# Softmax division moved from the rows of P to the weighed values in PSUM, with the prologue and the loads in another order

## The chip, the cores and the metric

The kernel runs on one core of one Trainium2 chip. The metric is the device time of one execution in microseconds (us), as the median of several runs. A profiled execution has a span, from its first to its last instruction, and a time of its own, a little longer than the span.

## The reference

`x` is 1024 rows (tokens) of 512 numbers. What is computed, cut to what matters:

```python
xn = _layernorm(x)                                     # 1024 x 512
qkv = xn @ w_qkv.T                                     # 32 query heads in 8 groups of 4, 8 key and 8 value heads, 128 wide
scores = einsum('bskgd,btkd->bkgst', qh, kh) / sqrt(128)
scores = where(causal, scores, finfo.min)
probs = softmax(scores, axis=-1)
attn = einsum('bkgst,btkd->bskgd', probs, vh)
s = attn.reshape(B, S, 4096) @ w_dense.T               # 1024 x 512
g = silu(ffn(xn))                                      # three 512 x 512 layers of weights +1 and -1
return x + s * g
```

## The kernel before, in words

Every fp32 product is made of three matmuls of fp32r parts: a value is split into a hi part (a rounding copy, by ACT) and a lo part (the value minus hi, by DVE or POOL), and `three` (lines 1074 to 1079) adds hi·hi, hi·lo and lo·hi. So each result that goes into another matmul is read by ACT (hi) and then by DVE or POOL (lo).

The work is in 8 groups, one for each key head with its 4 query heads. The program is a prologue (layer norm, its transposes, the projections of group 0 for the first 512 tokens, the first row block of scores), a loop of 7 bodies, and a last group, which also holds the feed-forward layers and the output. Each engine has its own list of items, run strictly in order: `prologue()`, `BODY` and `LAST` give those lists for PE (TensorE), ACT, DVE, POOL and SP, the queue that issues all DMAs. Semaphores tie the lists together. Nothing is scheduled at run time. An engine that waits holds up everything behind it in its list.

The items of a body, for 8 row blocks i of 128 tokens:

- `unit.p.half.c`: a quarter of a projection (q0 to q3, k, v), three matmuls of 512 columns into one of two shared PSUM banks. `split.p` makes the hi and lo parts of a loaded weight piece of 256 KB (lines 863 to 876, POOL 739 to 748); `load.p` brings it into a ring of 5 slots. The pieces are q0 to q3, k, v and wd0 to wd3 (`w_dense`).
- `scores.i.r`: scores of 32 tokens times 4 heads (128 rows) against the keys up to there, 32 to 1024 columns; r is 0 to 3. `max.i.r` (DVE, 927) masks them, negates them and takes the row's extreme; `exp.i.r` (ACT, 789) writes the row tile to `prob_even` or `prob_odd` and its sum to `row_sum`.
- `inverse.i.r` (DVE, 936) is the reciprocal of the sums; `norm.i.r` multiplies the tile by it in place: tiles 0 and 1 on ACT (798), 2 and 3 on POOL (729).
- `flip.i` (DVE, 945) transposes the 32 x 32 blocks. DMAs then bring the row block, tokens along the free dimension, into `pt_lo`: rows 1 to 3 and 8 by way of DRAM (`dw`, 640, and `dr`, 652), rows 4 to 7 by 16 small DMAs within SBUF (`move`, 663). Row 8 is row block 0 of the next group; the prologue makes it for group 0. `LAND_AFTER` says how many pairs must have been weighed before the slots of a row may be overwritten.
- `land.i.j`: hi (ACT, 833) and lo (POOL, 737; five pairs of a group on DVE, 996) of one 128 x 512 piece of P.
- `weigh.i.j` (PE): that piece times the values, added up over j in `ps_o`. `hi.weigh.i` (ACT, 839) and `lo.weigh.i` (DVE, 1009) split the sum; `dense.i.h` (PE) multiplies it by the piece of `w_dense`, and `lo.dense.i` (DVE, 1042) adds the product to `y`.

In the prologue POOL zeroes all of `y` (line 750, 128 x 4096). The last group ends with `dense.7`, its add into `y`, `gate.7`, `add_x.7` and the output DMA.

Of the kernel before, what the change touches and what calls it, by code (L numbers as in the profile page):

```python
# [123 lines left out]
def parse(tokens):  # L125


    def item(words):
# [4 lines left out]
    return [item(token.split(".")) for token in tokens.split()]


def prologue():
# [7 lines left out]
    pe = ln(0, 1, 2, 3) + unit("q0") + unit("q1") + ln(4, 5) + unit("q2") + ln(6, 7) \  # L144
        + unit("q3") + unit("k") + unit("v") + [("scores", first, r) for r in tiles] + values
# [18 lines left out]
    sp = [("load", p) for p in PIECES] + [("scales",), ("dw", first), ("dr", first)]
# [11 lines left out]
        dense.0.2 dense.0.3 scores.5.0 scores.5.1 weigh.2.1 weigh.2.2 unit.q2.0.0 unit.q2.0.1
        unit.q2.0.2 scores.5.2 scores.5.3 unit.q2.0.3 dense.1.0 dense.1.1 dense.1.2 scores.6.0
        dense.1.3 vblocks.1 weigh.3.0 weigh.3.1 weigh.3.2 weigh.3.3 scores.6.1 dense.2.0 dense.2.1
        dense.2.2 weigh.4.0 scores.6.2 weigh.4.1 scores.6.3 dense.2.3 weigh.4.2 unit.q0.0.0
        scores.7.0 scores.7.1 weigh.4.3 unit.q0.0.1 weigh.4.4 unit.q0.0.2 weigh.5.0 scores.7.2  # L180
        unit.q0.0.3 unit.q1.0.0 unit.q1.0.1 weigh.5.1 scores.7.3 weigh.5.2 unit.q1.0.2 unit.q1.0.3
# [12 lines left out]
        exp.3.3 norm.3.0 hi.unit.q3.1 norm.3.1 hi.land.1.0 hi.land.1.1 hi.split.q3 hi.split.v
        hi.weigh.0 hi.land.2.0 exp.4.0 hi.land.2.1 exp.4.1 hi.land.2.2 hi.weigh.1 norm.4.0 exp.4.2
        exp.4.3 norm.4.1 hi.split.k exp.5.0 exp.5.1 hi.weigh.2 hi.land.3.0 hi.land.3.1 hi.land.3.2
        hi.land.3.3 exp.5.2 hi.unit.q2.0 exp.5.3 norm.5.0 norm.5.1 hi.vblocks.1 hi.weigh.3
        hi.land.4.0 exp.6.0 hi.land.4.1 exp.6.1 hi.land.4.2 hi.land.4.3 hi.land.4.4 norm.6.0
# [143 lines left out]
class Run:  # L342
# [907 lines left out]
```

## Time and profile before

| | |
|---|---|
| device time, median of 3 runs | 947.64 us (946.23 to 949.11) |
| profiled execution: its own time | 945.07 us |
| profiled execution: span | 943.4 us |
| mean granted clock of TensorE | 0.991 |
| instructions | 15763 |
| start to start of two bodies | 106.9 us |

The profile gives each engine's busy time, a table by stretches of time, the waits with the engine that ended them, and a timeline of instructions. In a timeline row the first number is the start, the second how long it took; a matmul's length contains the filling of a pipeline, so that the distance from one start to the next tells what it costs. A bracket holds the idle time of the engine before the row and what ended it. SPq is the queue of SP, with the issues of DMAs.

### The profile page before, as it was taken

The numbers are of one execution on the slowest core, as the hardware profiler recorded it, in microseconds if no ns is written. First come the engines' busy times: TensorE is split into PE (matmuls) and PEld (weight loads), VectorE is DVE, ScalarE is ACT, GpSimd is POOL, SyncE is SP. The second block draws the span as 40 slices with busy tenths as digits, with TensorE's granted clock in tenths as the row PEclk, the third lists the DMA queues.
The fourth block names the chain that finished last, engine by engine and source line by source line (L and its number), as shares of the span: only waits on it lengthen the run. The fifth ranks groups of instructions, "written<-read, shape, count | busy, mean of one in ns | idle before, by whom it ended". The sixth has DMA issues, their size and how long they took to land.

```text
span 943.4 us, 15763 instructions
## 1 busy us (share of the span) xinstructions
PE 909.3 (96%) x4272; PEld 758.4 (80%) x4272; DVE 639.8 (68%) x1291; ACT 583.8 (62%) x1205; POOL 613.1 (65%) x500
## 2 busy tenths in 40 slices
PE   6879999999999999999999999999999999999997
PEld 5768777888788877888788877888788877888785
DVE  8447755787667765786667765777567775598646
ACT  3368654776558754777558664778457664656733
POOL 6058665677558764678467774678467774466947
PEclk9879999999999999999999999999999999999999
DMA  4066454755447454655447545555537546344335
GB/s 156 12 177 176 103 124 116 193 137 124 111 124 198 112 117 128 181 142 128 105 124 202 120 103 141 167 145 128 115 111 213 122 90 155 101 138 107 80 90 179
DMA packets 185463, 124.84 MB, mean 132 GB/s; under 512 B 12896, under 2 KB 161888, under 8 KB 185440
## 3 DMA queue, kind: packets, MB, share of 16 engines
q1 hardware_dynamic: 185440, 124.57, 51.3%
q8 instruction: 10, 0.16, 0.1%
q14 instruction: 13, 0.11, 0.0%
HBM read 46.93 MB, written 23.07 MB: 74 GB/s over the span
## 4 chain that ended last, share of the span: by engine, by line
POOL 41%; issue 40%; PE 10%; DVE 3%; SPq 2%; DMA 1%; ACT 1%; POOLq 1%; DVEq 0%; ACTq 0%
POOL pt_lo L737 23%; POOL prob_odd L729 5%; POOL w_lo L747 5%; POOL prob_even L729 4%; POOL wd_lo L747 3%; SPq L663 2%; PE ps_m L1209 2%; PE ps_m L1077 2%; PE ps_m L1078 2%; PE ps_m L1079 2%; PE ps_s L1077 1%; PE ps_s L1078 1%; PE ps_s L1079 1%; PE ps_o L1077 1%; DVE half_var L901 0%
## 5 line engine op out<-in xcount | busy, mean ns | idle before, releaser
L737 POOL TENSOR_TENSOR pt_lo<-pt_lo,pt_hi 128x512 fp32r<-128x512 f32 x248 | 332.7, 1366 | 117.1 <-ACT pt_hi L833 115.7
L927 DVE CUSTOM_DVE_ANT_0 ps_s<-ps_s,mask 128x32 f32<-128x32 f32 (+31 forms) x256 | 182.0, 714 | 102.9 <-PE ps_s L1079 98.3
L833 ACT ACTIVATE pt_hi<-pt_lo 128x512 fp32r<-128x512 f32 x288 | 170.0, 626 | 77.2 <-PE ps_o L1079 23.1
L1077 PE MATMUL ps_m<-xn_hi,w_hi 128*128 128x512 f32 (+1 forms) x388 | 153.3, 395 | 0.7 <-DVE xn_lo L1002 0.7
L1078 PE MATMUL ps_m<-xn_lo,w_hi 128*128 128x512 f32 (+1 forms) x388 | 151.8, 391 | 0.0
L1079 PE MATMUL ps_m<-xn_hi,w_lo 128*128 128x512 f32 (+1 forms) x388 | 151.6, 391 | 0.0
L1077 PE MATMUL ps_s<-k_hi,q_hi 128*128 128x480 f32 (+15 forms) x384 | 125.5, 327 | 9.2 <-ACT prob_odd L789 9.1
L1077 PE MATMUL ps_o<-pt_hi,v_hi 128*128 128x512 f32 x288 | 119.1, 413 | 8.8 <-POOL pt_lo L737 7.6
L1078 PE MATMUL ps_s<-k_lo,q_hi 128*128 128x480 f32 (+15 forms) x384 | 127.3, 332 | 0.0
L1079 PE MATMUL ps_s<-k_hi,q_lo 128*128 128x480 f32 (+15 forms) x384 | 127.1, 331 | 0.0
L729 POOL TENSOR_TENSOR prob_even<-prob_even,row_inv 128x96 f32<-128x96 f32 (+3 forms) x64 | 64.6, 1020 | 96.0 <-DVE row_inv L936 95.7
L789 ACT ACTIVATE prob_odd<-ps_s,neg_max 128x160 f32<-128x160 f32 (+15 forms) x128 | 95.8, 751 | 38.7 <-DVE neg_max L927 37.8
L789 ACT ACTIVATE prob_even<-ps_s,neg_max 128x32 f32<-128x32 f32 (+15 forms) x128 | 82.5, 645 | 56.5 <-DVE neg_max L927 52.7
L1078 PE MATMUL ps_o<-pt_lo,v_hi 128*128 128x512 f32 x288 | 113.0, 392 | 0.0
L1079 PE MATMUL ps_o<-pt_hi,v_lo 128*128 128x512 f32 x288 | 112.9, 392 | 0.0
L1077 PE MATMUL ps_m<-wd_hi,at_hi 128*128 128x512 f32 x256 | 100.4, 392 | 0.9 <-DVE at_lo L1009 0.9
L729 POOL TENSOR_TENSOR prob_odd<-prob_odd,row_inv 128x224 f32<-128x224 f32 (+3 forms) x64 | 77.8, 1235 | 35.5 <-DVE row_inv L936 35.5
L1078 PE MATMUL ps_m<-wd_lo,at_hi 128*128 128x512 f32 x256 | 99.9, 390 | 0.0
L1079 PE MATMUL ps_m<-wd_hi,at_lo 128*128 128x512 f32 x256 | 99.8, 390 | 0.0
L945 DVE STREAM_TRANSPOSE prob_odd<-prob_odd 128x1024 f32<-128x1024 f32 (+1 forms) x80 | 95.4, 1222 | 0.0
L1077 PEld LDWEIGHTS ps_s<-k_hi,q_hi 128*128 128x128 f32 x384 | 72.8, 190 | 19.6 <-ACT prob_odd L789 10.0
L1079 PEld LDWEIGHTS ps_m<-xn_hi,w_lo 128*128 128x128 f32 x388 | 73.4, 189 | 15.8
(103 smaller groups left out, 1624.4 us busy)
## 6 DMA issues: line engine op xcount, KB each, us to landing
pt_lo<-prob_odd SPq DMA_DIRECT2D x128, 128.0 KB, 2.4
pt_lo<-prob_even SPq DMA_DIRECT2D x128, 112.0 KB, 2.3
raw<-wqkv SPq DMA_DIRECT2D x48, 256.0 KB, 2.9
pt_lo<-prob_odd SPq DMA_DIRECT2D x128, 96.0 KB, 2.2
pt_lo<-prob_even SPq DMA_DIRECT2D x128, 80.0 KB, 2.1
raw<-wd SPq DMA_DIRECT2D x32, 256.0 KB, 3.5
turned<-prob_odd SPq DMA_DIRECT2D x32, 256.0 KB, 4.0
pt_lo<-turned SPq DMA_DIRECT2D x8, 1024.0 KB, 5.5
```

The source lines that it names most:

```text
L663: sp.dma_start(pt_lo[b * Q:(b + 1) * Q, slots, h * P:(h + 1) * P].bitcast(F32), prob_quadrants(i)[h * Q:(h + 1) * Q, :, b, :])\
L729: pool.tensor_tensor(rows, rows, row_inv[:, slot:slot + 1, None].to_broadcast([P, width(i % BLOCKS, tile) // Q, Q]), ALU.mult).then_inc(no ...
L737: pool.tensor_tensor(pt_lo[:, slot, :], pt_lo[:, slot, :].bitcast(F32), pt_hi[:, hi_slot, :], ALU.subtract).then_inc(land_lo, 1)
L747: pool.tensor_tensor(lo, raw[:, r.raw_slot(piece), :], hi, ALU.subtract)\
L789: act.activation(prob_tile(i, tile), as_tiles(score_row(i, tile)), ACT.Exp, scale=-1.0, bias=neg_max[:, slot:slot + 1], accum_out=row_sum[ ...
L833: act.activation(pt_hi[:, hi_slot, :], pt_lo[:, LAND_AT[i % BLOCKS] + j, :].bitcast(F32), ACT.Copy).then_inc(land_hi, 1)
L927: dve.tensor_tensor_reduce(out=scores, in0=scores, in1=mask[:, S - width(i % BLOCKS, tile):S], scale=-1.0, scalar=BIG, op0=ALU.add, op1=AL ...
L945: dve.transpose(rows, rows).then_inc(flipped, 1)
L1077: pe.matmul(out, sta_hi, mov_hi, start=start, stop=False)
L1078: pe.matmul(out, sta_hi, mov_lo, start=False, stop=False)
L1079: return pe.matmul(out, sta_lo, mov_hi, start=False, stop=stop)
L1209: mm = pe.matmul(bank[:, :], ffn_w[layer][c][:, o * P:(o + 1) * P], ffn_in(layer, part, c, half), start=(c == 0 and part == 0), stop=(c == ...
```

## The change

The rows of P are no longer normalized. `norm` is gone from ACT and POOL, 32 items a group. `inverse.i` is one reciprocal of the four sums of a row block. Its 128 x 4 result is written by `rw.i` to the DRAM tensor `inv`, and `rr.i` reads the 512 numbers back into each of the 128 partitions (`inv_rows`). A new DVE item, `mul.weigh.i`, multiplies the weighed sum in `ps_o` by them in place, before `hi.weigh.i` and `lo.weigh.i`. `flip.i` now waits for the row's four `exp` items alone.

```diff
-    if what == "norm":                                  (ACT; the same on POOL, as a tensor_tensor)
-        act.wait_ge(inverse_done, r.score_no(i, tile))
-        act.activation(rows, rows, ACT.Copy, scale=row_inv[:, slot:slot + 1])
-    dve.wait_ge(exp_done, r.score_no(i, tile))
-    dve.reciprocal(row_inv[:, slot:slot + 1], row_sum[:, slot:slot + 1])
+    dve.wait_ge(exp_done, r.score_no(i, TILES - 1))
+    dve.wait_ge(inv_written[i % 2], INV_WRITTEN0 + r.inv_writes(i) - 16)
+    dve.reciprocal(row_inv[:, stat_slots(i)], row_sum[:, stat_slots(i)])
+elif what == "rw":
+    sp.wait_ge(inverse_done, r.row_no(i))
+    sp.wait_ge(inv_landed, INV_LANDED0 + 16 * r.row_no(i - 2))
+    sp.dma_start(inv_d[i % 2, :, :], row_inv[:, stat_slots(i)])
+elif what == "rr":
+    sp.wait_ge(inv_written[i % 2], INV_WRITTEN0 + r.inv_writes(i))
+    sp.wait_ge(attn_scaled, r.row_no(i - 1))
+    sp.dma_start(inv_rows[:, :], inv_d[i % 2, :, :].rearrange("p r -> (p r)").partition_broadcast(P))
+if what == "mul":
+    dve.wait_ge(block_weighed, WEIGHED0 + PAIRS * g + tri(i + 1))
+    dve.wait_ge(inv_landed, INV_LANDED0 + 16 * r.row_no(i))
+    dve.tensor_tensor(weighed_f32(i).rearrange("p h (r c) -> p h r c", c=Q),
+        ps_o[i % 2][:, :].rearrange("p (h r c) -> p h r c", r=TILES, c=Q),
+        inv_rows[:, :].rearrange("p (h c r) -> p h r c", c=Q, r=TILES), ALU.mult)
-    act.wait_ge(block_weighed, WEIGHED0 + PAIRS * g + tri(i + 1))     (hi.weigh)
+    act.wait_ge(attn_scaled, BLOCKS * g + i + 1)
```

In the prologue POOL zeroes only the first of the 8 blocks of `y`, at its very start, and a DMA copies it to the other seven. Query projection q2 comes ahead of the transposes of blocks 4 and 5, q3 ahead of those of 6 and 7. The pieces wd0 to wd3 of a group are loaded at the end of the group before (in the prologue for group 0).

```diff
-    pe = ln(0, 1, 2, 3) + unit("q0") + unit("q1") + ln(4, 5) + unit("q2") + ln(6, 7) + unit("q3") + unit("k") + unit("v")
+    pe = ln(0, 1, 2, 3) + unit("q0") + unit("q1") + unit("q2") + ln(4, 5) + unit("q3") + ln(6, 7) + unit("k") + unit("v")
-        pool.memset(y[:, :, :], 0.0)
+        pool.memset(y[:, 0, :], 0.0).then_inc(y_zero, 1)
+        sp.wait_ge(y_zero, 1)
+        sp.dma_start(y[:, 1:BLOCKS, :], y[:, 0:1, :].to_broadcast([P, BLOCKS - 1, E])).then_inc(y_zero, 16)
-    sp = [("load", p) for p in PIECES] + [("scales",), ("dw", first), ("dr", first)]
+    sp = [("load", p) for p in PIECES + [f"wd{h}" for h in range(HEADS)]] + [("scales",), ("dw", first), ("rw", first), ("dr", first), ("rr", first)]
```

The tables `BODY` and `LAST` are written anew for all five engines. The head of PE's table for a body shows how:

```diff
-        scores.1.0 unit.q2.1.0 scores.1.1 scores.1.2 unit.q2.1.1 scores.1.3 unit.q2.1.2 scores.2.0
+        scores.1.0 scores.1.1 unit.k.1.0 scores.1.2 scores.1.3 unit.k.1.1 scores.2.0 unit.k.1.2
```

Three places of the order, before and after (line numbers are those of each kernel). The first is SP at the end of the prologue, up to the first weight loads of the loop. Before:

```order
L632 DMA scales<-s 128x1 x3
L640 DMA turned<-prob_even 32x4x128 x4
L652 DMA pt_lo<-turned 128x512
L671 UNCONDITIONAL_BRANCH
L671 ISA
L628 ISA
L628 DMA raw<-wd 128x512
```

With the change:

```order
L629 DMA raw<-wd 128x512 x4
L634 DMA y<-y 128x7x512
L637 DMA scales<-s 128x1 x3
L660 DMA turned<-prob_even 32x4x128 x4
L644 DMA inv<-small 128x4
L672 DMA pt_lo<-turned 128x512
L652 DMA inv_rows<-inv 128x512
```

The four loads of `wd` stood behind the way of row 8 over DRAM and now stand ahead of it, with the copy of `y`; `inv` and `inv_rows` are new.

The second is DVE in the prologue, from the statistics of blocks 4 to 7 (the `TENSOR_TENSOR xn_lo` rows are the lo parts of the transposed blocks, `q_lo` those of the projections). Before:

```order
L950 BN_STATS bn<-prob_odd 128x6 x4
L896 BN_AGGR mv<-bn 128x2 x4
...
L1026 SCALAR_TENSOR_TENSOR q_lo<-ps_m,q_hi 128x16x32
L958 TENSOR_SCALAR prob_odd<-prob_odd,mv,rstd 128x512 x4
L1026 SCALAR_TENSOR_TENSOR q_lo<-ps_m,q_hi 128x16x32
L1002 TENSOR_TENSOR xn_lo<-ps_s,xn_hi 128x4x128 x2
```

With the change:

```order
L967 BN_STATS vt<-prob_odd 128x6 x4
L1042 SCALAR_TENSOR_TENSOR q_lo<-ps_m,q_hi 128x16x32
L903 BN_AGGR vt<-vt 128x2 x4
...
L1042 SCALAR_TENSOR_TENSOR q_lo<-ps_m,q_hi 128x16x32
L975 TENSOR_SCALAR prob_odd<-prob_odd,vt 128x512 x4
L1042 SCALAR_TENSOR_TENSOR q_lo<-ps_m,q_hi 128x16x32
L1019 TENSOR_TENSOR xn_lo<-ps_s,xn_hi 128x4x128 x2
```

The lo parts of q0 and q1 moved ahead of the work that they followed.

The third is SP in a body, between the last move of row 4 and the first of row 5 (8 and 12 DMAs of the same rows left out). Before:

```order
L663 DMA pt_lo<-prob_even 32x5x128 x4
L657 REGISTER_ALU
L660 REGISTER_ALU
L663 DMA pt_lo<-prob_odd 32x6x128 x4
```

With the change:

```order
L683 DMA pt_lo<-prob_even 32x5x128 x4
L652 DMA inv_rows<-inv 128x512
L641 REGISTER_ALU
L643 ISA
L644 DMA inv<-small 128x4
L677 REGISTER_ALU
L680 REGISTER_ALU
L683 DMA pt_lo<-prob_odd 32x6x128 x4
```

The read of row 3's reciprocals (`rr.3`) and the write of row 4's (`rw.4`) now stand between the two.

## Rows read from the trace of the kernel before

**Rows 1.** The page: busy time, share and instructions of each engine.

```profile
PE 909.3 (96%) x4272; PEld 758.4 (80%) x4272; DVE 639.8 (68%) x1291; ACT 583.8 (62%) x1205; POOL 613.1 (65%) x500
```

**Rows 2.** Stretches: prologue, then one body; columns in the first line.

```profile
core 0: us, PE busy (x) PEld busy (x) DVE busy (x) ACT busy (x) POOL busy (x), PEclk, DMA share, GB/s
20.00:40.00 20.00, 15.64 (x73) 13.30 (x73) 11.36 (x20) 5.26 (x9) 3.14 (x2) 0.83 0.00 1
40.00:60.00 20.00, 10.94 (x52) 9.70 (x52) 7.33 (x38) 9.84 (x34) 6.82 (x8) 0.74 0.44 133
161.40:268.30 106.90, 106.21 (x502) 88.52 (x501) 73.28 (x151) 69.89 (x146) 71.85 (x57) 1.00 0.55 137
```

**Rows 3.** Timeline of POOL, DVE and PE, 17 to 29 us, the first stall.

```profile
19.10 3.52 POOL L750 MEMSET y<- 128x4096 f32 x1
17.98 4.66 DVE L901 TENSOR_SCALAR half_var<-var_eps 128x4 f32<-128x4 f32 x1
24.36 1.97 PE L1099 MATMUL ps_s<-ident,prob_odd 128*128 128x128 f32 x8 [4.98 <-DVE prob_odd L958]
...
28.68 0.40 PE L1077 MATMUL ps_m<-xn_hi,w_hi 128*128 128x512 f32 x1
28.91 0.40 PE L1078 MATMUL ps_m<-xn_lo,w_hi 128*128 128x512 f32 x1
```

**Rows 4.** Timeline of ACT, DVE, SPq and PE, 41 to 54 us, the second stall.

```profile
41.77 0.19 ACT L789 ACTIVATION_READ_ACCUMULATOR prob_even<-ps_s,neg_max 128x1 f32 x1
43.09 0.70 DVE L945 STREAM_TRANSPOSE prob_even<-prob_even 128x512 f32<-128x512 f32 x1
43.82 1.80 SPq L640 DMA_DIRECT2D turned<-prob_even  x4
46.95 0.34 SPq L652 DMA_DIRECT2D pt_lo<-turned  x1
49.48 0.63 ACT L833 ACTIVATE pt_hi<-pt_lo 128x512 fp32r<-128x512 f32 x1 [6.59 <-DMA pt_lo<-turned]
50.54 1.18 ACT L876 ACTIVATE wd_hi<-raw 128x512 fp32r<-128x512 f32 x2 [0.42 <-DMA raw<-wd]
52.50 0.63 ACT L876 ACTIVATE wd_hi<-raw 128x512 fp32r<-128x512 f32 x1 [0.78 <-DMA raw<-wd]
53.56 0.61 PE L1077 MATMUL ps_s<-k_hi,q_hi 128*128 128x288 f32 x1 [9.06 <-ACT prob_odd L789]
```

**Rows 5.** Timeline of PE in the second body, two places where a weigh is late.

```profile
221.62 0.39 PE L1079 MATMUL ps_m<-xn_hi,w_lo 128*128 128x512 f32 x1
222.01 0.50 PE L1077 MATMUL ps_o<-pt_hi,v_hi 128*128 128x512 f32 x1
...
260.79 0.40 PE L1079 MATMUL ps_o<-pt_hi,v_lo 128*128 128x512 f32 x1
261.35 0.50 PE L1077 MATMUL ps_o<-pt_hi,v_hi 128*128 128x512 f32 x1 [0.15 <-POOL pt_lo L737]
```

**Rows 6.** Timeline of SPq in the second body: the moves of rows 5 and 7.

```profile
207.72 10.51 SPq L663 DMA_DIRECT2D pt_lo<-prob_odd  x16
...
240.90 10.60 SPq L663 DMA_DIRECT2D pt_lo<-prob_odd  x16
```

**Rows 7.** Waits of PE in the last group, 803.5 to 943.4 us (total, times, longest).

```profile
PE ps_o L1077 <- POOL pt_lo L737: 2.2, 2, 1.6
PE ps_m L1077 <- DVE at_lo L1009: 0.9, 1, 0.9
PE ps_m L1209 <- DVE y L1042: 0.8, 1, 0.8
```

**Rows 8.** Groups of instructions: busy us, mean ns of one, idle before and its releaser.

```profile
L729 POOL TENSOR_TENSOR prob_even<-prob_even,row_inv 128x96 f32<-128x96 f32 (+3 forms) x64 | 64.6, 1020 | 96.0 <-DVE row_inv L936 95.7
L996 DVE TENSOR_TENSOR pt_lo<-pt_lo,pt_hi 128x512 fp32r<-128x512 f32 x40 | 55.8, 1395 | 16.5 <-ACT pt_hi L833 16.4
L1026 DVE SCALAR_TENSOR_TENSOR q_lo<-ps_m,q_hi 128x512 fp32r<-128x512 f32 x64 | 43.8, 684 | 48.4 <-ACT q_hi L849 48.4
```

More of the change, by code:

```diff
@@ L176 @@
[L176 to L181, printed above, removed]
@@ L194 @@
[L194 to L198, printed above, removed]
-        exp.6.2 exp.6.3 norm.6.1 hi.land.5.0 exp.7.0 hi.land.5.1 exp.7.1 hi.land.5.2 hi.land.5.3
@@ L219 @@
[L219 to L221 removed]
+        max.1.0 max.1.1 max.1.2 max.1.3 max.2.0 max.2.1 flip.1 max.2.2 lo.unit.k.1 max.2.3
+        inverse.1 max.3.0 max.3.1 flip.2 lo.unit.q1.1 max.3.2 inverse.2 max.3.3 lo.unit.q3.1
+        mul.weigh.0 flip.3 lo.unit.q0.1 lo.weigh.0 lo.unit.q2.1 inverse.3 mul.weigh.1 max.4.0
+        max.4.1 lo.unit.v.1 lo.weigh.1 max.4.2 max.4.3 lo.dense.0 flip.4.0 flip.4.1 flip.4.2
@@ new lines @@
+        max.5.0 max.5.1 flip.4.3 mul.weigh.2 inverse.4 max.5.2 max.5.3 lo.weigh.2 lo.dense.1
+        flip.5.0 flip.5.1 max.6.0 mul.weigh.3 flip.5.2 max.6.1 flip.5.3 lo.unit.q3.0 lo.weigh.3
+        max.6.2 inverse.5 max.6.3 lo.dense.2 lo.vblocks.1 flip.6.0 flip.6.1 max.7.0 mul.weigh.4
+        flip.6.2 max.7.1 lo.weigh.4 lo.dense.3 flip.6.3 inverse.6 max.7.2 max.7.3 lo.dense.4
+        flip.7.0 flip.7.1 lo.land.6.4 lo.unit.q2.0 mul.weigh.5 flip.7.2 lo.weigh.5 lo.land.6.1
+        flip.7.3 lo.unit.k.0 inverse.7 lo.unit.q1.0 lo.unit.q0.0 max.8.0 max.8.1 max.8.2
@@ L222 @@
+        mul.weigh.6 max.8.3 lo.land.7.1 lo.unit.v.0 lo.weigh.6 flip.8 lo.land.7.4 lo.dense.5
+        inverse.8 lo.land.7.7 lo.vblocks.0 mul.weigh.7 lo.weigh.7 lo.dense.6 lo.dense.7
     """,
     "pool": """
-        lo.split.wd0 lo.split.wd1 lo.split.wd2 norm.1.2 norm.1.3 norm.2.2 lo.split.wd3 norm.2.3
-        lo.split.q0 lo.split.q1 lo.split.q2 norm.3.2 norm.3.3 lo.land.1.0 lo.land.1.1 lo.split.q3
-        lo.land.2.0 lo.land.2.1 lo.land.2.2 lo.split.v norm.4.2 norm.4.3 lo.split.k lo.land.3.0
@@ new lines @@
+        inverse.1 max.3.0 flip.2 lo.unit.q3.1 max.3.1 inverse.2 max.3.2 lo.unit.q0.1 max.3.3
+        lo.unit.q2.1 mul.weigh.0 flip.3 lo.unit.k.1 lo.weigh.0 inverse.3 max.4.0 lo.unit.v.1
+        max.4.1 build.0 max.4.2 lo.dense.0 mul.weigh.1 max.4.3 lo.weigh.1 build.1 lo.hidden.0.0.0
+        lo.hidden.0.0.1 max.5.0 max.5.1 flip.4.0 flip.4.1 flip.4.2 lo.hidden.0.0.2 flip.4.3
+        max.5.2 lo.hidden.0.0.3 max.5.3 inverse.4 mul.weigh.2 build.2 max.6.0 lo.dense.1
+        lo.weigh.2 flip.5.0 flip.5.1 lo.hidden.1.0.0 flip.5.2 max.6.1 lo.hidden.1.0.1 flip.5.3
@@ new lines @@
+        max.6.2 lo.hidden.1.0.2 mul.weigh.3 max.6.3 lo.dense.2 lo.weigh.3 inverse.5 max.7.0
+        flip.6.0 lo.vblocks.1 max.7.1 flip.6.1 mul.weigh.4 flip.6.2 flip.6.3 lo.weigh.4 max.7.2
+        lo.hidden.1.0.3 max.7.3 inverse.6 lo.hidden.0.1.0 flip.7.0 lo.hidden.0.1.1 flip.7.1
+        lo.hidden.0.1.2 flip.7.2 lo.dense.3 flip.7.3 inverse.7 lo.land.6.4 mul.weigh.5
+        lo.hidden.0.1.3 lo.weigh.5 lo.land.6.1 lo.dense.4 lo.hidden.1.1.0 lo.hidden.1.1.1
+        lo.hidden.1.1.2 lo.hidden.1.1.3 lo.land.7.1 mul.weigh.6 gate.0 lo.weigh.6 gate.1
```

358 lines of the change are left out of this document (172 added, 186 removed).

## The prediction

> **What bounds the kernel now.** I read the shares of the engines first, then the stretches, then the timeline of PE wherever it stood still, and last the timelines of whoever let it go. PE is busy for 909.3 of 943.4 us, and no other engine for more than 68% [rows 1]. So work taken from ACT, POOL or DVE is worth nothing by itself; only PE's idle and slow time can be won. The change leaves PE's matmuls as they are, in number and size, and orders them anew.
>
> PE loses time in four places.
>
> - In the prologue it waits 4.98 us for the transposes' input [rows 3]. The reader should see that a DVE instruction on 128 x 4 numbers lasts 4.66 us and ends at 22.64, just after POOL's clearing of `y` (19.10 to 22.62). When PE goes on, it runs at 1.2 GHz for 4.3 us, from 24.36 to 28.68; from there on a 512-wide matmul follows the one before after 0.23 us [rows 3]. The granted clock of 20 to 40 us is 0.83 [rows 2].
> - At 44.5 us it waits 9.06 us for the first `exp` of the loop, and the granted clock of 40 to 60 us is 0.74 [rows 2, 4].
> - In a body it is busy for 106.2 of 106.9 us at full clock [rows 2]. The distances from start to start show a bit more: 0.39 and 0.56 us where 0.23 would do, so 0.16 and 0.33 us lost [rows 5]. A body has five such places ahead of a weigh, of which these are the first and the last, and together they lose 1.6 us.
> - In the last group it waits 2.2, 0.9 and 0.8 us [rows 7].
>
> **The first stall of the prologue.** POOL's clearing shrinks from 4096 to 512 columns and lies at its start. The 4.66 us instruction then ends earlier, by 3.5 us (the clearing's length) at least and by 4.5 if nothing of it is its own, and the scaled blocks are ready at 19.9 to 20.9 instead of 24.4. The lo parts of q0 and q1 now come first, which costs DVE twice 0.68 us [rows 8]: 21.2 to 22.2. PE no longer needs them then, since the 12 matmuls of q2 (12 x 0.23 = 2.7 us) carry it from 19.3 to 22.0. I take the whole 4.98 us, and half of the 4.3 slow us, 2.2: **7.2 us**. The copy of `y` by DMA is 1.8 MB. It is issued when the fifth weight piece is split, near 18 us; at the 137 GB/s that a body moves [rows 2] it takes 13 us and ends near 31. DVE needs it, and the scales that stand behind it on SP, at about 32.5 (39.7 now, less 7.2). I cost it at nothing; the cover is 1 to 2 us thin, and behind it the price is one for one.
>
> **The second stall.** The chain is: last `exp` of row 8 (ends 41.96), flip, write to DRAM, read, hi part of the landed piece, three splits of `wd`, first `exp` of the loop [rows 4]. The flip started 1.1 us after that `exp`; it no longer waits for reciprocals and norms: 1.1 us less. The splits waited 0.42 and 0.78 us for loads that stood behind row 8 on SP and are now long done: 1.2 us less. The new `rw.8` is issued within the 1.3 us in which SP waits for the write anyway, so it costs nothing. PE has one unit quarter less to do before it stalls (3 x 0.23 = 0.7 us), which it does after instead. The clock drops all the same. 1.1 + 1.2 - 0.7: **1.6 us**.
>
> **The bodies.** Removed in a body: 16 norms on POOL of 1.0 us and more [rows 8], at least 16 us, and as many on ACT; 24 of 32 small reciprocals. Added on DVE: 8 multiplications of 512 columns. The trace of before has no multiplication with a PSUM output; from below it is bounded by 0.68 us (PSUM and SBUF in, SBUF out), from above by 1.40 us (the lo part of a landed piece, which shares its time with POOL) [rows 8]. Of its two inputs only one is in SBUF, as in the 0.68 us row, so I take 0.7: 5.6 us a body, on an engine that is idle for 34 of 107 us [rows 2].
>
> The Trainium skill, page "SBUF — State Buffer", section "Door 1: The DMA port swizzle", says that SBUF is read in lines of 16 bytes and that every access that goes to a new line is penalized. The new multiplication reads `inv_rows` in steps of four fp32, so each element would be a new line. By that rule the sum would have more than 0.7 us for each multiplication; it gives no figure, and no row here has such a read. It is a rival below.
>
> What is a weigh late for? Not for the norms alone. The moves of a row wait on SP until its slots are free (for row 7, until the third pair of row 6 is weighed). Then 16 issues take 10.5 or 10.6 us [rows 6], and 14.3 us after the first of them PE starts the row's first weigh (row 5: 207.72 to 222.01) [rows 5, 6]. So what counts is how much PE work lies between the pair that frees the slots and the first weigh of the row. Counted in matmuls of 0.23 us (score tiles by their widths), that is before and after: row 4 14.9 and 14.4, row 5 14.2 and 15.8, row 6 14.3 and 16.3, row 7 14.3 and 15.7 us. Rows 6 and 7 get 1.4 to 2 us more, which clears their four stalls. For row 4 its flips, not the slots, decided before, and two norms in a row on POOL (2 x 1.0 us) are gone ahead of them, more than the 0.5 us lost. Row 5 is still close: the slots of row 4 are free at 32.3 us of the body, so SP is in its moves until 43; then come `rr.3` and `rw.4` with some 0.45 us each (a write to DRAM has 1.80 us for four [rows 4]), so the moves of row 5 start at 43.8 and its weigh at 58.1, where PE is there at 57.7: 0.4 us late. Of 1.6 us 0.4 stay: **1.2 us a body, 8.4 in seven**.
>
> **The new waits.** `mul.weigh.i` waits for `rr.i`, and behind it on DVE stand flips and maxima. Row 3 is the worst: its last weigh ends at 41.7 us of the body, but `rr.3` is issued only at 43 and lands some 2.5 us later, as a read of the same 256 KB did (46.95 to 49.48 [rows 4]). So DVE stands for some 4 us. Behind it are `flip.5.2`, which SP needs at 49, and `max.6.1`, whose scores are ready only at 46.3. I cost this wait at nothing, with 1 us to spare. At the end of a group `dense.7` starts 2.7 us after the last weigh; multiplication, hi and lo take 0.7 + 0.6 + 0.7 and their handovers 0.3: 0.4 us to spare.
>
> **The last group** loses 3.9 us [rows 7]. The way of row 7 grows from 14.3 to 17.1 us, which clears its 1.6 us; the waits for `at_lo` and `y` came of products that stood right behind their inputs, and 18 to 28 us lie there now. The final steps (add, gate, add, store) are unchanged. With DVE and PE in a new order something small will come up elsewhere: **3.3 us**.
>
> **Sum.** 7.2 + 1.6 + 8.4 + 3.3 = 20.5 us. The profiled execution took 945.07 us, so 924.6 by its own time. The median of the runs before is 2.6 us above that execution: 927 us.
>
> **Rivals.**
>
> - *The body keeps its stalls* (20%). Late pieces come from the 16 issues of a row on SP, and the change puts 16 more DMAs a group on SP. For it: SP's moves of rows 4 and 5 are back to back. Against: rows 6 and 7 have SP idle before them. Then 7.2 + 1.6 + 3.3 = 12.1 us are won: 935.5.
> - *The strided read is slow* (8%). At 1.4 us each the chain to `dense.7` is 0.3 us too long in each of 8 groups, the other rows have room: 929.5. The Trainium skill's page "SBUF — State Buffer" would have this one come.
> - *The clearing only changes hands* (8%): the copy of `y`, with the scales behind it, lands late and holds DVE's first maximum. At 5 us late the first stall is back in another place: 932. Against: 40 to 60 us is where DMAs were busy, 20 to 40 had none [rows 2].
> - *Slower than before* (5%): `mul.weigh.3` waits longer than said for `rr.3`, queued behind 16 moves, and DVE, held in order, feeds PE late with maxima, lo parts and flips. It has 1 us to spare; it decides once the row is late by more than 1 us, and the whole is slower once a group loses over 20.5 / 8 = 2.6 us, so from 3.6 us late. At 5 us late: 8 x 4 = 32 lost, 959.
> - *The prologue does not do what it says* (4%): DVE's long instruction had another cause than the clearing. Then 7.2 us stay: 934.
>
> The forecast has 55%. The low end is all that PE can get: 7.2 + 1.6 + 11.5 (7 x 1.65) + 3.9, and 2.9 for the slow clock after the second stall, my estimate from the 0.74 [rows 2]: 27.1, so 920.5, and 2.5 below for the spread of runs. The high end takes in the kept stalls with one of the two prologue rivals. Range 918 to 940. A measurement of this kernel can tell 0.3%, some 3 us, from no change. Faster by more: all cases but the slower one and a bit: 0.92. Same: 0.03. Slower: 0.05.
>
> **What would show it.** PE at 19 to 22 us without a gap, and granted clock 1.0 for 20 to 36 us. The wait for the first `exp` of the loop at about 7.5 us and starting near 36. A body of 105.7 us. DVE idle some 4 us ahead of the multiplication of row 3, released by `inv_rows`, with no wait of PE behind it. ACT and POOL below 52% busy. The multiplication at 0.7 us. The prediction is wrong where a body is above 107 us or PE waits for DVE in it.

## The result and the profile after the change

The changed kernel takes 943.17 us (median of 12 runs, 935.63 to 948.52), the kernel before beside it 947.12 us (946.16 to 950.03). The ratio is 0.9955, 95% interval 0.9938 to 0.9972: faster by a small amount that is clear of the noise, 4 us where 20 were forecast, and 3 us above the range. The profiled execution took 943.73 us, its span is 941.5. Three of the runs told of below, one each of `a3`, `b1` and `c2`, took 1005, 2441 and 1505 us for no cause that is known; the ratios leave them out.

In the page POOL has shrunk to 49% as forecast; ACT stands at 54%, where less than 52 was said. PE is busy for 905.5 us against 909.3 [rows 1], so it has gained little. The page's busy times:

```profile
PE 905.5 (96%) x4272; PEld 761.8 (81%) x4272; DVE 664.4 (71%) x1163; ACT 509.4 (54%) x1077; POOL 464.4 (49%) x372
```

Two stretches of the prologue and one body (376.91 to 484.40), with the columns in the first line:

```profile
core 0: us, PE busy (x) PEld busy (x) DVE busy (x) ACT busy (x) POOL busy (x), PEclk, DMA share, GB/s
20.00:40.00 20.00, 18.34 (x104) 15.52 (x102) 13.43 (x40) 7.67 (x19) 1.87 (x3) 1.00 0.42 131
40.00:60.00 20.00, 13.36 (x56) 11.51 (x57) 8.09 (x21) 10.17 (x29) 6.25 (x5) 0.83 0.51 119
376.91:484.40 107.49, 105.25 (x501) 88.76 (x500) 77.55 (x135) 60.80 (x130) 53.61 (x41) 1.00 0.61 156
```

The first stall of the prologue is gone: from 20 to 40 us the granted clock is 1.00 where it was 0.83 [rows 2], and PE has no wait there. Not all of this is won: ahead of it, at 11.86 us, PE now waits 3.68 us for its first scaled blocks of x (1.34 before), and the granted clock of 0 to 20 us is 0.91 where it was 1.00. The body is no shorter than before (107.5 against 106.9), though ACT and POOL do 9 and 18 us less in it.

The waits of PE in the whole changed kernel, and one of ACT for DMAs, say where it went (engine, tile and line, what it waited for: us in total, times, longest).

```profile
PE ps_o L1094 <- POOL pt_lo L753: 15.2, 11, 5.4
PE ps_s L1094 <- ACT prob_odd L805: 8.3, 1, 8.3
ACT pt_hi L841 <- DMA pt_lo<-turned: 65.5, 24, 9.0
```

The same wait of ACT in the kernel before:

```profile
ACT pt_hi L833 <- DMA pt_lo<-turned: 9.6, 9, 6.6
```

ACT waits 65.5 us for pieces that come back from DRAM, where it waited 9.6. One body's timeline shows which piece (start, us, engine, line; in brackets the idle time before and what ended it):

```profile
402.36 0.32 SPq L652 DMA_DIRECT2D inv_rows<-inv  x1
402.93 1.50 SPq L629 DMA_DIRECT2D raw<-wd  x3
404.63 0.38 SPq L672 DMA_DIRECT2D pt_lo<-turned  x1
...
413.55 2.19 ACT L841 ACTIVATE pt_hi<-pt_lo 128x512 fp32r<-128x512 f32 x4 [6.23 <-DMA pt_lo<-turned]
414.26 5.02 POOL L753 TENSOR_TENSOR pt_lo<-pt_lo,pt_hi 128x512 fp32r<-128x512 f32 x4 [6.97 <-ACT pt_hi L841]
...
415.58 0.50 PE L1094 MATMUL ps_o<-pt_hi,v_hi 128*128 128x512 f32 x1 [2.19 <-POOL pt_lo L753]
```

It is row 3, the last and largest row that goes through DRAM. Its read (`dr.3`, 1 MB) is issued 27.7 us into the body, right behind three loads of `wd` for the next group (256 KB each) and a broadcast of reciprocals (256 KB), and ACT takes the piece 8.9 us later. ACT has stood for it since 407.3, POOL for ACT, PE for POOL. The text ahead of the prediction says that `wd` is loaded "at the end of the group before"; the table has these loads in the middle of SP's list, 26 us into a body of 107, where the kernel before had them at its head. Every body has this wait: PE idles 5.41 us in the first, with the granted clock at 0.50 for 6.8 us from 87.5 on, and 1.67, 1.19, 2.19, 0.48, 0.40 and 1.52 us in the others. The DMA issues of the changed kernel (count, KB each, median us to landing):

```profile
inv_rows<-inv SPq DMA_DIRECT2D x64, 256.0 KB, 3.5
raw<-wd SPq DMA_DIRECT2D x32, 256.0 KB, 5.1
turned<-prob_odd SPq DMA_DIRECT2D x32, 256.0 KB, 5.0
pt_lo<-turned SPq DMA_DIRECT2D x8, 1024.0 KB, 7.7
```

And three of these rows in the kernel before, where all of them land sooner:

```profile
raw<-wd SPq DMA_DIRECT2D x32, 256.0 KB, 3.5
turned<-prob_odd SPq DMA_DIRECT2D x32, 256.0 KB, 4.0
pt_lo<-turned SPq DMA_DIRECT2D x8, 1024.0 KB, 5.5
```

The span can be cut at the first `scores` matmul of each body in PE's timeline. The first body begins at 40.82 us before and 35.34 after. Before and after: up to PE's resumption behind the second stall 53.56 and 46.64, **6.9 us won**; from there to the second body 107.8 and 114.3, **6.5 lost**; six bodies 642.2 and 643.3, **1.1 lost**; the rest 139.9 and 137.3, **2.6 won**. That is 1.9 us, the difference of the spans (943.4 and 941.5). Of the 6.9 us, 0.7 are only put off: the changed kernel resumes with one quarter of a projection less done, and pays it in the first body.

### The profile page after: what moved, and what is told of

It reads as the page before. It is cut to its first block, busy times and chain, and to the rows that moved or that the text cites. A ratio compares the mean times of both kernels' runs of the same rounds, so it can differ in the third digit from the quotient of the medians.

```text
span 941.5 us, 15708 instructions
## 1 busy us (share of the span) xinstructions
PE 905.5 (96%) x4272; PEld 761.8 (81%) x4272; DVE 664.4 (71%) x1163; ACT 509.4 (54%) x1077; POOL 464.4 (49%) x372
## 4 chain that ended last, share of the span: by engine, by line
issue 46%; PE 25%; POOL 25%; SPq 1%; DVE 1%; DMA 1%; ACT 1%; POOLq 0%; DVEq 0%
POOL pt_lo L753 17%; POOL w_lo L763 4%; PE ps_m L1094 3%; PE ps_m L1095 3%; PE ps_m L1096 3%; POOL wd_lo L763 3%; PE ps_m L1226 2%; PE ps_o L1094 2%; PE ps_s L1094 2%; PE ps_o L1096 2%; PE ps_o L1095 2%; PE ps_s L1095 2%; PE ps_s L1096 2%; SPq L683 1%; PE ps_s L1211 1%
## 5 line engine op out<-in xcount | busy, mean ns | idle before, releaser
L753 POOL TENSOR_TENSOR pt_lo<-pt_lo,pt_hi 128x512 fp32r<-128x512 f32 x248 | 328.1, 1347 | 397.3 <-ACT pt_hi L841 396.9
L841 ACT ACTIVATE pt_hi<-pt_lo 128x512 fp32r<-128x512 f32 x288 | 169.8, 626 | 116.9 <-DMA pt_lo<-turned 65.5
L1094 PE MATMUL ps_s<-k_hi,q_hi 128*128 128x480 f32 (+15 forms) x384 | 128.3, 334 | 9.4 <-ACT prob_odd L805 8.3
L1094 PE MATMUL ps_o<-pt_hi,v_hi 128*128 128x512 f32 x288 | 115.4, 401 | 15.2 <-POOL pt_lo L753 15.2
L805 ACT ACTIVATE prob_odd<-ps_s,small 128x160 f32<-128x160 f32 (+15 forms) x128 | 95.2, 747 | 51.8 <-DVE small L934 50.5
L805 ACT ACTIVATE prob_even<-ps_s,small 128x32 f32<-128x32 f32 (+15 forms) x128 | 82.5, 646 | 65.6 <-DVE small L934 60.8
L962 DVE STREAM_TRANSPOSE prob_odd<-prob_odd 128x1024 f32<-128x1024 f32 (+1 forms) x80 | 97.5, 1233 | 5.4 <-ACT prob_odd L805 5.4
L951 DVE TENSOR_TENSOR ps_o<-ps_o,inv_rows 128x512 f32<-128x512 f32 x64 | 68.7, 1073 | 26.9 <-PE ps_o L1096 22.9
L1094 PEld LDWEIGHTS ps_m<-xn_hi,w_hi 128*128 128x128 f32 x388 | 73.5, 189 | 12.2 <-DVE q_lo L1042 0.8
```

Of the source, the lines that this page charges most:

```text
L753: pool.tensor_tensor(pt_lo[:, slot, :], pt_lo[:, slot, :].bitcast(F32), pt_hi[:, hi_slot, :], ALU.subtract).then_inc(land_lo, 1)
L805: act.activation(prob_tile(i, tile), as_tiles(score_row(i, tile)), ACT.Exp, scale=-1.0, bias=neg_max[:, slot:slot + 1], accum_out=row_sum[ ...
L841: act.activation(pt_hi[:, hi_slot, :], pt_lo[:, LAND_AT[i % BLOCKS] + j, :].bitcast(F32), ACT.Copy).then_inc(land_hi, 1)
L951: dve.tensor_tensor(weighed_f32(i).rearrange("p h (r c) -> p h r c", c=Q), ps_o[i % 2][:, :].rearrange("p (h r c) -> p h r c", r=TILES, c= ...
L962: dve.transpose(rows, rows).then_inc(flipped, 1)
L1094: pe.matmul(out, sta_hi, mov_hi, start=start, stop=False)
```

## The experiments

Two theories stood at the start. *Theory 1*: the read of row 3 is late because of the `wd` loads ahead of it on the DMA engines. *Theory 2*: SP comes to it too late. A third blames the broadcasts. All times are medians of 5 runs or more. The runs of one letter went on one chip, with the kernel before beside them (946.50 us with `a`, 946.70 with `b`, 946.12 with `c`, 947.58 with `d`); the ratios are against that. "Body" is the mean of the six bodies from the second on in the profiled execution: 107.0 us before, 107.2 after.

**The wd loads behind the read** (`a1_wd_behind_dr3`), in the body's table of SP:

```diff
-  rr.2 load.wd0 load.wd1 load.wd2 dr.3 load.wd3 move.4.0
+  rr.2 dr.3 load.wd0 load.wd1 load.wd2 load.wd3 move.4.0
```

> The changed kernel, with the three wd loads that SP issues ahead of dr.3 put behind it; nothing else. Theory 1 (the turned row 3 lands late, 8.8 us after its issue, because 768 KB of wd are on the DMA engines when it starts): it lands in some 5.5 us and is issued 1.5 us earlier, PE's wait of 1 to 2.3 us ahead of the first weigh of row 3 goes, and the time falls by 8 to 16 us, to 927 to 935. Theory 2 (SP comes to the read late, whatever is loaded): the read still takes over 8 us, the wait shrinks only by the 1.5 us of the earlier issue, and 3 to 6 us are won. Theory 3 (the broadcasts of the reciprocals congest the DMA engines): no change, 941 to 945.

930.03 us (927.9 to 932.0), ratio 0.9818 [0.9797, 0.9839]; body 106.1, the first body 118.7 instead of 125.6. The same place in this kernel:

```profile
392.81 0.37 SPq L672 DMA_DIRECT2D pt_lo<-turned  x1
393.43 2.19 SPq L629 DMA_DIRECT2D raw<-wd  x4
398.49 2.20 ACT L841 ACTIVATE pt_hi<-pt_lo 128x512 fp32r<-128x512 f32 x4 [2.11 <-PE ps_o L1096]
399.20 5.06 POOL L753 TENSOR_TENSOR pt_lo<-pt_lo,pt_hi 128x512 fp32r<-128x512 f32 x4 [2.87 <-ACT pt_hi L841]
```

ACT's last wait is now PE's ring, the piece was there before: it landed in 5.7 us at most, from an issue 0.9 us earlier in the body. Over all bodies the read takes 6.4 us in the median (7.7 with the change). PE's wait for row 3 is gone in all of them. Moving three loads won 13 us, within the 8 to 16 of theory 1, about half of it in the first body; theory 2 in its own terms (a read of over 8 us, 3 to 6 us won) falls. The earlier issue is a part of the gain all the same, and this run does not separate it from the faster landing; `b3` below has the faster landing alone. Counted as the prediction counts, from start to start beyond 0.23 us, PE loses 0.4 to 0.9 us ahead of `weigh.5.0`, where 0.4 was said.

**The wd loads far away** (`a2_wd_before_move6`): all four between `rw.5` and `move.6.0`.

> The changed kernel, with all four wd loads moved out of the part around row 3 to SP's idle time ahead of the moves of row 6. Theory 1: as with the loads behind dr.3 or better, since the moves of row 4 are also free of them: 925 to 934, no wait of PE for row 3 over 0.5 us, bodies of 105.5 to 106. Theory 2: 3 to 6 us won. Theory 3: no change. If the loads collide with the moves of row 6 instead, a wait of PE comes up ahead of the first weigh of row 6 and most of the gain is given back.

930.54 us, 0.9821 [0.9800, 0.9841], body 106.1. The same gain, and no new wait ahead of row 6; the first body alone waits 2.17 us ahead of `weigh.5.0`.

**The read first** (`a3_dr3_first`):

```diff
-  dw.3 load.v rw.3 rr.2 load.wd0 load.wd1 load.wd2 dr.3 load.wd3
+  dw.3 dr.3 load.v rw.3 rr.2 load.wd0 load.wd1 load.wd2 load.wd3
```

> The changed kernel, with dr.3 issued right behind dw.3, ahead of the load of v, the write and the broadcast of reciprocals and the four wd loads, which then follow it closely. Theory 1: the read starts on free DMA engines but the loads join it 2 us later; it lands in 6 to 8 us, from an issue 2 us earlier, so at least 2.5 us earlier in all: the wait ahead of row 3 goes, 8 to 14 us won. Theory 2 (issue time alone): the same 8 to 14 us, with the landing still over 8 us long. A price is possible: the broadcast of row 2 comes 2 us later and the multiplication of row 2 could hold DVE; then a wait of PE for at_lo of row 2 shows.

959.25 us, 1.0128 [1.0103, 1.0154], body 110.2: 16 us slower than the changed kernel, where both theories had expected a gain. The read lands in 5.6 us, so that part held. The price was not at row 2's multiplication but at the load of `v`, the `raw<-wqkv` here:

```profile
405.62 0.39 SPq L672 DMA_DIRECT2D pt_lo<-turned  x1
406.27 0.37 SPq L629 DMA_DIRECT2D raw<-wqkv  x1
...
411.87 0.63 ACT L883 ACTIVATE w_hi<-raw 128x512 fp32r<-128x512 f32 x1 [5.76 <-DMA raw<-wqkv]
412.40 0.75 ACT L805 ACTIVATE prob_even<-ps_s,small 128x608 f32<-128x608 f32 x1
...
413.30 0.66 PE L1094 MATMUL ps_s<-k_hi,q_hi 128*128 128x352 f32 x1 [2.36 <-ACT prob_even L805]
```

The read may be issued only when the write of row 3 has landed; SP stood for that from 400.0, when its last write was issued, to 405.62, and the load of `v` went out 29.1 us into the body, where the changed kernel has it at 23.4. ACT, in its order, stood for the split of `v`, and behind it were the exps that free PE's banks.

**The factors read in order** (`a4_contiguous_factors`): `"p (h c r) -> p h r c"` in the multiplication becomes `"p (h r c) -> p h r c"`.

> The changed kernel, with the multiplication reading inv_rows in order instead of in steps of four numbers; each value is then multiplied by the reciprocal of another row of the tile. Theory A (the 1.07 us of the multiplication are the strided read of SBUF): it takes 0.65 to 0.75 us. Theory B (they are the PSUM output or the two inputs): it stays at 1.0 to 1.1 us. For the whole time theory 1 expects little of it either way, 0 to 2 us less, since DVE is idle for a third of a body.

The multiplication's group in the changed kernel (busy us, mean ns of one, idle before and its releaser):

```profile
L951 DVE TENSOR_TENSOR ps_o<-ps_o,inv_rows 128x512 f32<-128x512 f32 x64 | 68.7, 1073 | 26.9 <-PE ps_o L1096 22.9 <-DMA inv_rows<-inv 4.0
```

And with this edit:

```profile
L951 DVE TENSOR_TENSOR ps_o<-ps_o,inv_rows 128x512 f32<-128x512 f32 x64 | 44.7, 698 | 23.7 <-PE ps_o L1096 21.3 <-DMA inv_rows<-inv 2.5
```

The stride costs 375 ns. The 16-byte line rule of the Trainium skill, page "SBUF — State Buffer", section "Door 1: The DMA port swizzle", is what the prediction named for this; the trace agrees in direction, and gives the size. The whole took 939.15 us (928.82 to 939.96), 4 us less than the changed kernel; but row 3 is late here too (3.18 us in the first body, then 0.61 to 2.48; body 107.4), so the whole time does not say what the stride costs; `d2` below asks again.

**The clearing back on POOL** (`b1_clear_on_pool`): `memset` of all of `y` where the changed kernel clears block 0, and no copy by DMA.

> The changed kernel, with the whole of y cleared by POOL, at the place where the changed kernel clears its first block, and without the copy by DMA. If the clearing held DVE in the prologue as the prediction said: the clearing now lies at the start of POOL's work, ahead of its splits, lasts some 3.5 us and delays the first lo of the weights by that much; 2 to 5 us slower than the changed kernel. If the clearing had cost nothing: within 0.3% of it.

939.03 us, 0.9917 [0.9899, 0.9935]: neither; 4 us faster. In the profile the first body begins 0.9 us later than in the changed kernel (36.24 and 35.34), so nothing is won in the prologue; the gain is in the waits for row 3 (3.14 us in the first body instead of 5.41; body 106.6). POOL clears all of `y` from 5.42 to 8.93 us here. So once the clearing stands at the start of POOL's list, its size matters little: 0.9 us at the start of the first body.

**The same on the mended kernel** (`c1_wd_behind_clear_pool`): `a1` with that clearing.

> The kernel with the wd loads behind dr.3, and the whole clearing of y on POOL in place of the copy by DMA. Alone on the changed kernel this clearing won 4 us. If that came from the prologue, it is won here too: 926. If it came from the row 3 race in the bodies (which differs from run to run), it is gone here, and what stays is the 0.9 us by which the first body began later: 930 to 932.

929.71 us, against 930.03: the same, and the first body 0.7 us later (36.09 against 35.42). The gain of `b1` was the row 3 wait coming out smaller, for a reason that no run shows; the copy of `y` costs nothing and wins nothing that the whole time shows.

**The kernel before with the small clearing alone** (`b2_before_small_clear`): its `zero_y` clears one block, a DMA copies it to the other seven.

> The kernel before, with POOL clearing one block of y instead of eight and a DMA copying it to the other seven; nothing else. Prediction's first step: DVE's 4.66 us instruction shrinks to under 1.2 us, PE's wait of 4.98 us goes, and 5 to 7 us are won: 940 to 943. Rival (the DVE instruction had another cause): no change, 945 to 948. Rival (the copy lands late and holds DVE's first maximum): 2 to 4 us won, with a longer second stall.

942.37 us, 0.9958 [0.9942, 0.9973]: 4.3 us, a bit under the expected 5 to 7. DVE's instruction and POOL's clearing:

```profile
19.66 1.68 DVE L905 TENSOR_SCALAR half_var<-var_eps 128x4 f32<-128x4 f32 x1
20.79 0.53 POOL L754 MEMSET y<- 128x512 f32 x1
...
23.07 1.12 PE L1104 MATMUL ps_s<-ident,prob_odd 128*128 128x128 f32 x8 [1.76 <-DVE prob_odd L962]
```

4.66 us has become 1.68, and PE's wait 1.76 instead of 4.98 [rows 3]. In both kernels the instruction ends 0.02 us after POOL's clearing: the first step of the prediction had the right cause. By itself it is worth as much as the whole change (0.9958 and 0.9955).

**Tiny broadcasts** (`b3_tiny_broadcast`): each `rr` writes 4 numbers a partition instead of 512, so the products are no longer divided by their sums.

> The changed kernel, with each broadcast of reciprocals cut from 256 KB to 16 bytes for each partition; all else issued and waited for as before. The products are then multiplied by ones and a few reciprocals instead of by the reciprocals. Theory 3 (the 16.8 MB of broadcasts congest the DMA engines): the turned row 3 lands in some 5.5 us instead of 8.8, and 8 us or more are won. Theory 1 (the wd loads do it): landing of row 3 still over 7.5 us, 0 to 4 us won.

930.58 us, 0.9829 [0.9809, 0.9850], body 106.0. The read of row 3 takes 6.5 us in the median (7.7 with the change, 6.4 in `a1`), though the `wd` loads stand where the change has them and the read is issued as late as there (27.7 to 28.4 us into a body from the second on; 27.7 to 29.2 with the change). So theory 3's prediction of the gain held too: taking 0.25 MB of broadcasts from ahead of the read helps as much as taking 0.75 MB of loads. The late landing has both as its cause. With the broadcasts gone PE still waits 2.45 us for row 3 in the first body, and 0.62 at most in the others.

**Room on ACT and POOL taken away** (`c2_splits_twice`): on `a1`, every split of a weight piece in a body is done twice.

> The kernel with the wd loads behind dr.3, and in a body each of the ten splits of a weight piece done twice on ACT and twice on POOL, with the same result: some 6 us more on ACT and 13 us more on POOL in a body, about what the norms took there before. If only PE's late pieces count and the room on ACT and POOL is worth nothing by itself: within 3 us of 930. If the change lives from that room: the ring of splits ahead of rows 2 and 3 runs late on POOL, weighs of rows 2 and 3 wait, 8 us or more are lost, 938 or above.

991.66 us, 1.0479 [1.0458, 1.0499], body 114.6: 8.5 us more in a body than in `a1`. PE waits 1.4 us ahead of `scores.2.0`, 1.5 to 1.8 ahead of `unit.v.1.0`, 1.6 ahead of `weigh.3.0` and 0.3 to 0.5 for each piece of row 2. "Work taken from ACT, POOL or DVE is worth nothing by itself" does not hold as a general sentence: the room counts at the places where the splits stand in a block. The run does not show what the norms cost where they stood before, since they were spread over the body.

**Row 3 wanted later** (`c4_weigh3_later`), on the changed kernel's table of PE:

```diff
-  dense.1.2 weigh.3.0 scores.5.2 scores.5.3 dense.1.3 weigh.3.1
+  dense.1.2 scores.5.2 scores.5.3 dense.1.3 weigh.3.0 weigh.3.1
```

> The changed kernel, its DMAs untouched, with weigh.3.0 put behind scores.5.2, scores.5.3 and dense.1.3 on PE, so that row 3 is wanted 2.6 us later. Theory 1 and 3 alike (the turned row 3 lands up to 3 us too late for the new order of PE): the wait ahead of it goes in all bodies but the first, 8 to 12 us are won, 931 to 936. If PE's wait there had another cause (ACT or POOL behind in their own work), it moves along with the weigh: no change, 941 to 945.

950.8 us, 1.0047 [1.0024, 1.0070]: slower still. The profiled execution is the fastest of twelve, 945.65 us, with a body of 108.1, and it shows that the wait has only changed its name:

```profile
406.82 2.19 ACT L841 ACTIVATE pt_hi<-pt_lo 128x512 fp32r<-128x512 f32 x4 [6.10 <-DMA pt_lo<-turned]
...
408.92 0.80 ACT L805 ACTIVATE prob_odd<-ps_s,small 128x672 f32<-128x672 f32 x1
...
409.86 0.45 PE L1094 MATMUL ps_s<-k_hi,q_hi 128*128 128x384 f32 x1 [3.08 <-ACT prob_odd L805]
```

ACT stands in its order for the landing, and the exps of row 5 are behind it; now the scores come first on PE, and they need these exps. PE waits for them in every body, 1.4 to 3.1 us from the second on. The deadline of the landing is ACT's, not PE's.

**Two small moves on the mended kernel** (`c3_row5_and_tail`): `a1`, and

```diff
-  weigh.4.4 weigh.5.0 scores.7.1 dense.3.1 weigh.5.1     (body, PE)
+  weigh.4.4 dense.3.1 weigh.5.0 scores.7.1 weigh.5.1
-  lo.land.7.3 add_x.0 add_x.1 lo.land.7.5 lo.land.7.6     (last group, POOL)
+  lo.land.7.3 lo.land.7.5 lo.land.7.6 add_x.0 add_x.1
```

> The kernel with the wd loads behind dr.3, and two small moves: in a body dense.3.1 goes ahead of weigh.5.0 on PE, so that the row's first weigh is wanted 0.68 us later; in the last group POOL makes the lo parts of the pieces 7.5 and 7.6 ahead of its first two additions of x instead of behind them. The wait of 0.35 to 0.9 us ahead of weigh.5.0 shrinks by 0.68 us in each body, 2 to 4 us in seven, and of the 2.1 us ahead of weigh.7.5 and 7.6 most goes: 924 to 927. If the additions of x were what sets the end, up to 2 us are given back.

**924.16 us** (923.62 to 926.83), 0.9769 [0.9751, 0.9788]: the fastest complete version of this study, 22 us below the kernel before. The wait ahead of `weigh.5.0` is 0.1 us at most, but the body gains only 0.1 us (106.0): in two bodies PE now waits 0.4 to 0.6 us for exps instead. Most of the 6 us are in the last group, which took 138.9 us in `a1` (137.4 in `a2`, 136.8 in `c1`) and takes 135.0 here. It has no such wait left; in `a1` its additions of x had waited for blocks of x from DRAM, with the pieces 7.5 and 7.6 behind them on POOL:

```profile
902.97 3.09 POOL L772 TENSOR_TENSOR y<-y,prob_even 128x512 f32<-128x512 f32 x2 [3.22 <-DMA prob_even<-x]
906.02 2.94 POOL L753 TENSOR_TENSOR pt_lo<-pt_lo,pt_hi 128x512 fp32r<-128x512 f32 x2
```

Four more runs were to settle what stood open.

> The kernel with the wd loads behind dr.3 and the two small moves (924 us), with each broadcast of reciprocals cut from 256 KB to 16 bytes for each partition. If the broadcasts cost only by making row 3 late, and the place of the wd loads has mended that: within 2 us of 924. If 16.8 MB more on the DMA engines also cost elsewhere (pieces of the other rows, the second stall): 3 us or more below, 921 or less.

923.80 us, 0.9745 [0.9726, 0.9764], body 105.5: no difference from `c3` (0.9769 [0.9751, 0.9788]) that is clear of the noise. With the loads out of the way the 16.8 MB of broadcasts cost little; 2 us are not excluded.

> The same kernel (924 us), with the multiplication reading inv_rows in order, 0.70 us instead of 1.07; each value is then multiplied by the reciprocal of another row. If DVE has the room that the prediction gave it: within 2 us of 924. If 0.37 us on the way from the last weigh to at_lo count in each body: 1 to 3 us less, 921 to 923.

923.66 us, 0.9743 [0.9724, 0.9762], body 105.1: here too no difference that is clear of the noise. The rival of the slow strided read was half right: the read is slow, but its 375 ns cost the whole at most some 2 us. That they lie off the path altogether is likely and not shown.

`d3_before_with_copies` and `d4_c3_with_copies` put this ahead of `dr.3` in a body:

```diff
+ for h in range(3):
+     sp.dma_start(junk_d[g, h], wd_d[g, h]).then_inc(extra, 16)
```

> The kernel before, with three extra copies of 256 KB (wd, DRAM to DRAM, read by nobody) issued by SP in each body right ahead of the read of the turned row 3. If it is PE's new order that made the landing of row 3 count (the first weigh of row 3 stands 43 us into a body before, 36 us after the change): the read lands 3 us and more later and within 4 us of 946 nothing is lost. If ACT, which stands in order for that landing, holds exps or hi parts of others: 1 to 3 us a body, 953 to 970.

990.23 us, 1.0435 [1.0405, 1.0466], body 113.0, 20 us more than I had allowed. The read takes 9.4 us in the median instead of 5.5, and is issued 2.5 us later in the body, since SP issues the copies first:

```profile
428.76 2.22 SPq L655 DMA_DIRECT2D junk<-wd  x3
431.02 0.58 SPq L658 DMA_DIRECT2D pt_lo<-turned  x1
440.30 2.19 ACT L839 ACTIVATE pt_hi<-pt_lo 128x512 fp32r<-128x512 f32 x4 [5.94 <-DMA pt_lo<-turned]
...
443.39 0.45 PE L1083 MATMUL ps_s<-k_hi,q_hi 128*128 128x416 f32 x1 [3.37 <-ACT prob_odd L795]
```

PE's waits for ACT's exps grow from 9.1 us, once, to 36.2 us in eight places, and the granted clock drops at five of the seven new ones: the mean granted clock of the run is 0.972 (0.991 before). The later issue and the slower landing are not separated.

> The kernel at 924 us with the same three copies ahead of the read of the turned row 3. Theory 1: this brings the changed kernel's row 3 back; the read takes 8 us or more, PE waits 1 to 5 us ahead of weigh.3.0 in each body, 10 to 25 us are lost, 934 to 949. If the DMA engines had room: 926 or less.

953.35 us, 1.0072 [1.0044, 1.0101], body 109.6, 29 us more than `c3` and 4 more than I had allowed; PE waits 1.4 to 3.7 us ahead of `weigh.3.0`.

So the kernel before was just as near the edge. In its body at 375.18 the read is issued at 405.17, 30.0 us in, lands within 5.5, and ACT takes the row at 410.73, 35.6 us in, with no wait at all:

```profile
398.44 3.11 SPq L640 DMA_DIRECT2D turned<-prob_odd  x4
405.17 0.38 SPq L652 DMA_DIRECT2D pt_lo<-turned  x1
410.25 0.59 ACT L839 ACTIVATE at_hi<-ps_o 128x512 fp32r<-128x512 f32 x1
410.73 2.19 ACT L833 ACTIVATE pt_hi<-pt_lo 128x512 fp32r<-128x512 f32 x4
```

PE's first weigh of row 3 comes only at 43.3, which looks like 5 us of room; there is none, because ACT's queue stands between. What protected the old kernel was that nothing had been issued for 3.6 us ahead of this read.

## Why the prediction was wrong, step by step

- **The first stall (7.2 us): the cause right, the size not shown.** `b2` shows the cause and is worth 4.3 us. The first body begins at 35.34 instead of 40.82, 5.5 us earlier. This pair of profiles is a weak measure: PE's wait for its first scaled blocks of x, 3.68 us here and 1.34 before, lies between 2.1 and 4.2 in the other profiles with this prologue, and their first bodies begin at 34.5 to 36.7; in `d3`, whose prologue is that of the kernel before, the wait is 2.85 us and the first body begins at 43.96. What makes it vary was not tried; it is 3.42 in `b2`, with the old loads and the old order. DVE's instruction still takes 1.28 us, to 21.37, where POOL's splits end at 21.34.
- **The copy of `y`: right to cost it at nothing**, as `c1` shows. It landed in 8.4 us, not 13.
- **The second stall (1.6 us): half of it.** From the last exp of row 8 to PE it was 11.6 us, now 10.2 (36.47 to 46.64): 1.4 us less where 2.3 were said, so 0.7 after the quarter of a projection that is paid later; PE's wait shrank from 9.06 to 8.30. Flip and splits gained what was said, but the read of row 8 landed in 3.6 us instead of 2.5.
- **The bodies (8.4 us): the step that failed.** The four late weighs of rows 6 and 7 are gone from the second body on. But the argument "what counts is how much PE work lies between the pair that frees the slots and the first weigh" was made for rows 4 to 7 only. Row 3 has no moves; it waits for a read from DRAM. The change pulled ACT's use of it from 35.6 to 30.4 us and PE's from 43.3 to 36.3, and put a megabyte of other traffic right ahead of its read, which the sum left at nothing. Had I gone through every row this way, the term was in the tables and in the trace: three loads and a broadcast ahead of a read that already landed exactly on time. In place of 8.4 us won, the first body lost 5.8 (the 6.5 less the quarter put off) and the six others 1.1. Put right (`a1`), the kernel wins 13 us more; its six bodies take 106.1 us each, where 105.7 was forecast, and what is missing is row 5, 0.4 to 0.9 us late instead of 0.4. The sign of being wrong that was named, a body above 107 us, came (107.2).
- **The first body** lost most, since a wait of 5.41 us also took the clock down; this too is the wait for row 3.
- **New waits on DVE: right that they cost nothing.** DVE waits 2.0 to 2.8 us ahead of the multiplication of row 3 in the bodies of `a1` (4 forecast), and nothing of PE's hangs on it. The 0.7 us was the lower of two bounds and 1.07 was measured, with no effect clear of the noise (`d2`).
- **The last group (3.3 us): 2.6.** What stayed were the pieces 7.5 and 7.6, behind POOL's additions of x; `c3` won them.
- **The rivals.** "The body keeps its stalls" named the right term and the wrong mechanism: too many issues on SP. The slower one, a wait for `rr.3` with DVE held in order, did not come; its kind did, on ACT, for a DMA that I had not put on the list. `a3` shows it in full: a step that waits was moved past a load on SP, and the kernel was slower than before. The range had a fault of its own: kept stalls together with a prologue that does not do what it says would give 942.7 us, above its high end of 940.

Most of the 20.5 us were there: `a1`, with three loads moved, is 16 us below the kernel before, and `c3`, with two moves more that were not in the change, 22. The forecast of the sign held, by little: the small clearing alone, put into the kernel before, brings the same 4 us (`b2`), so that all the rest of the change comes out near nothing. The range did not hold, because the sum had no term for a DMA that becomes late.

## What to carry to other kernels

When a change moves PE's work forward, list every transfer that feeds it, with issue, landing and the moment at which the engine that first touches it (here ACT, two steps ahead of PE) comes to it in its own order; a landing that today coincides with its use has no slack, whatever the matmul behind it shows. Loads for later work go behind the read that someone is waiting for, unless they are themselves due. And a queue step that waits is moved past others only after asking who needs those.

## What the runs showed of the hardware

- The same read of 1 MB took 5.5, 6.4, 7.7 and 9.4 us in the median, with different transfers issued just ahead of it (before: nothing for 3.6 us; `a1`: a broadcast; the changed kernel: that and three loads; `d3`: three copies within DRAM). In the last group of the changed kernel, where neither loads nor a broadcast stand just ahead of it, it took 5.6.
- A fp32 multiplication of 128x512 with a PSUM operand and output takes 698 ns with the SBUF operand in order and 1073 ns in steps of four.
- DVE's instruction on 128x4 numbers ended within 0.03 us of the end of POOL's work in the kernel before, `b2` and the changed kernel: 22.64 (clearing to 22.62), 21.34 (clearing to 21.32), 21.37 (splits to 21.34). The first of them began at 17.98, ahead of the clearing, during a split, and lasted through the rest of that split and all of the clearing.
- The kernels in which PE waits for a DMA's landing spread more: 12 runs of the changed kernel lie within 12.9 us, 12 of the kernel before beside them within 3.9, five of `a1` within 4.1 and five of `c3` within 3.2.
